# Decoder layer on one core: the row maximum moves into the scores' own contraction, the gate into four column tiles, and TensorE's order becomes a cycle

## What is computed

```python
q = hidden_states @ Wq.T + bq          # k, v alike
scores = einsum('bhqd,bhkd->bhqk', q, k) * SCALE
attn = softmax(where(mask, scores, -inf), axis=-1)
return einsum('bhqk,bhkd->bhqd', attn, v) @ Wo.T + bo
```

```python
gp = softmax(xf @ gate_w.T, axis=-1)           # 8 experts
ew, _ = top_k(gp, 2)
ew = ew / (sum(ew) + 1e-09)
ef = silu(xf @ up_w.T) @ down_w.T              # 1024 wide
out = ef * sum(ew)
```

## Time and profile before

| what | value |
|---|---|
| median of 3 runs | 3605.91 us |
| lowest, highest | 3600.19, 3607.89 us |
| span of the profiled execution | 3601.5 us |
| PE busy | 3488.3 us, 97% of the span |
| DVE, POOL, ACT busy | 77%, 70%, 48% |
| share of PE in the chain that ended last | 93% |

### The profile page before, as it was taken

One profiled execution on the slowest core, in us unless ns is written; L12 is line 12 of the kernel. 1 busy time (PEld: TensorE's weight loads), 2 busy tenths in 40 slices (PEclk: granted clock), 3 DMA queues, 4 the chain that ended last, 5 costly groups with the idle time before them and its releaser, 6 DMA issues.

```text
span 3601.5 us, 97036 instructions
## 1 busy us (share of the span) xinstructions
PE 3488.3 (97%) x38789; PEld 2853.8 (79%) x38789; DVE 2764.0 (77%) x6256; ACT 1715.7 (48%) x4049; POOL 2507.6 (70%) x3159
## 2 busy tenths in 40 slices
PE   6699999999999999999999999999999999999998
PEld 5578888888888888888888888888888888888876
DVE  5677787787787787787787877877877877877863
ACT  2345545545545445445545545445445455455443
POOL 5767777777777677677677777777677677677742
PEclk8899999999999999999999999999999999999999
DMA  5111111111121121121121121111111111111100
GB/s 177 48 50 59 61 67 53 66 69 48 67 72 45 67 74 45 67 74 45 67 74 45 67 73 46 67 67 53 67 63 57 67 60 60 67 57 62 67 8 10
DMA packets 87098, 221.54 MB, mean 62 GB/s; under 512 B 8262, under 2 KB 53634, under 8 KB 70274
## 3 DMA queue, kind: packets, MB, share of 16 engines
q1 hardware_dynamic: 86658, 215.34, 16.9%
HBM read 164.92 MB, written 50.39 MB: 60 GB/s over the span
## 4 chain that ended last, share of the span: by engine, by line
PE 93%; DVE 4%; ACT 2%; issue 1%; POOL 0%; DMA 0%; SPq 0%; DVEq 0%; ACTq 0%
PE ps L869 13%; PE ps L860 13%; PE ps L722 11%; PE ps L700 10%; PE ps L839 9%; PE ps L756 8%; PE ps L811 8%; PE ps L788 6%; PE ps L728 5%; PE ps L680 3%; PE ps L780 3%; PE ps L849 2%; DVE held L1355 1%; PE ps L750 1%; ACT rest L1002 1%; DVE nmax_pair L1292 1%
## 5 line engine op out<-in xcount | busy, mean ns | idle before, releaser
L1124 POOL TENSOR_TENSOR chunks<-v_windows,xT 128x560 f32<-128x560 f32 (+1 forms) x384 | 870.8, 2284 | 259.0 <-DVE xT L1267 155.0
L1292 DVE TENSOR_REDUCE nmax_pair<-ps 128x4 f32<-128x480 f32 (+2 forms) x1280 | 776.1, 669 | 167.8 <-PE ps L756 167.5
L1119 POOL TENSOR_TENSOR chunks<-rest,k_windows 128x512 f32<-128x512 f32 (+1 forms) x384 | 552.9, 1455 | 436.8 <-DVE xT L1246 232.6
L969 ACT ACTIVATE prob<-ps 128x256 f32<-128x256 f32 (+2 forms) x1536 | 670.0, 548 | 331.9 <-PE ps L788 331.9
L860 PE MATMUL ps<-xT,w_up 128*128 128x256 f32 x2048 | 483.7, 384 | 0.0
L869 PE MATMUL ps<-w_down,held 128*128 128x256 f32 x2048 | 458.9, 382 | 1.8 <-DVE held L1355 1.6
L869 PEld LDWEIGHTS ps<-w_down,held 128*128 128x128 f32 x2048 | 383.9, 190 | 72.2 <-issue 20.4
L860 PEld LDWEIGHTS ps<-xT,w_up 128*128 128x128 f32 x2048 | 375.7, 191 | 44.7 <-issue 0.9
L1246 DVE TENSOR_REDUCE xT<-chunks 128x32 f32<-128x512 f32 (+1 forms) x384 | 294.0, 766 | 128.0 <-POOL chunks L1119 128.0
L927 ACT COPY xT<-ps 128x512 f32<-128x512 f32 x256 | 149.8, 585 | 489.3 <-PE ps L680 489.2
L1136 POOL TENSOR_SCALAR_AFFINE_SELECT prob<-prob 128x512 f32<-128x512 f32 x512 | 319.5, 655 | 75.7 <-ACT prob L969 75.7
(11 more groups left out here) (146 smaller groups left out, 6086.6 us busy)
## 6 DMA issues: line engine op xcount, KB each, us to landing
k_windows<-passed_on SPq DMA_DIRECT2D x64, 1024.0 KB, 4.6
v_windows<-passed_on SPq DMA_DIRECT2D x64, 1024.0 KB, 5.1
x<-in_x SPq DMA_DIRECT2D x64, 256.0 KB, 2.9
passed_on<-rest SPq DMA_DIRECT2D x64, 256.0 KB, 2.0
passed_on<-held SPq DMA_DIRECT2D x64, 256.0 KB, 2.0
out<-x SPq DMA_DIRECT2D x64, 256.0 KB, 2.1
y<-in_ctx SPq DMA_DIRECT2D x64, 120.0 KB, 2.8
w_up<-in_up SPq DMA_DIRECT2D x1, 1024.0 KB, 8.8
```

Source lines behind the costliest of these rows:

```text
L969: last = nc.scalar.activation(prob_pair(seq, L, m)[0:keys, :, r, col:col + qs], of_pair, ACT.Exp, scale=SCALE)
L1119: last = nc.gpsimd.tensor_tensor(chunk_of(c).rearrange("p (j d) -> p j d", d=D), q_row, window("k", (b + first) * D, (D, n), (1, D)), ALU. ...
L1124: last = nc.gpsimd.tensor_tensor(chunk_of(c).rearrange("p (h i j) -> p h i j", i=HD, j=WINDOW), window("v", b * D + first * HD, (HD, n), ( ...
L1292: nc.vector.tensor_reduce(nmax[s][:, tb, heads], src, AX_X, ALU.max, negate=True).then_inc(emptied[b], 1)
```

## The change

Per sequence:

- `kT` becomes two tiles for each attention, one per e: rows of the other head are scaled to zero by `half`, and one of these empty rows is set to 1 by a bias (`one_row`, or `bias_k[e]`). ACT writes k twice: 2 instructions instead of 1 for the causal k, 4 instead of 2 for the cross k.
- The matmuls with `pick` are gone, and with them `round_max`, its bf16 tiles and the constant. `shift` now transposes the fp32 maxima (128x16 in, 16x128 out), DVE copies 16 rows of 256.
- A new SP step `place` copies these rows by two DMAs (8 rows of 1 KB each) into the empty row of each quarter of `qT[e]`. `scores` waits for both. So the negated maximum enters as the 17th row of the fp32 contraction; the matmuls k by q stay as many and as large as they were.
- `gate` has the weights as its stationary operand, 32 columns in each of four column tiles, and streams 64 tokens through each: 8 matmuls for 4. DVE turns the result with a transpose instead of a copy.
- `Plan` orders PE's steps by `POSITION`, a number for each step within a cycle plus the number of the sequence; PE takes the next step of that line and no other, except at the ends (`FILLING`, `LOOKS`). The other engines' steps are due by the PE steps that follow them, shifted by `SHIFTED`. The two first score units of a layer may not be taken between those of another.

```diff
-DELAY = {("gate", None, "PE"): 55, ("project", 2, "PE"): 2975, ("project_out", 1, "PE"): -85,
...
+POSITION = {("turn", (0,)): -0.0773, ("turn_ctx", ()): -0.0394, ("project_rows", ("k",)): -0.0389, ("project_rows",
...
+            a = through("shift", (layer,), 0.2, "DVE", 0.4, last)
+            shifted = part("place", (layer,), "SP", 2 * DMA_ISSUE, [a], lag=2.0)
...
-            ready[parts[i].engine].append((SENIORITY * n - left[i] + delay[i], n, i))
...
+        line = sorted((n + due[i], n, i) for n, i in todo if parts[i].engine == "PE")
...
+                    elif name == "place":
+                        L, = args
+
+                        wait_taken(sp, "shift", seq, L)
+                        for e in range(2):
+                            to = qT[s][e][16 * (1 - e):P:32]
+                            sp.dma_start(to, nmaxT[s][8 * e:8 * e + 8, :]).then_inc(placed[s], 16)
...
-                        to = ps[:, b, :].bitcast(BF16)
                         for tb in range(2):
-                            last = nc.tensor.transpose(to[:, tb * P:(tb + 1) * P], nmax_parts[s][:, tb, :],
-                                                       ident_b[:])
+                            last = nc.tensor.transpose(ps[0:H, b, tb * P:(tb + 1) * P], nmax[s][:, tb, :], ident[:])
...
-                        wait_taken(pe, "shift", seq, L)
+                        pe.wait_ge(placed[s], reached["placed", "place", seq, (L,)])
...
-                                nc.tensor.matmul(ps[0:keys, to[r], n * qs:(n + 1) * qs], pick[rows, g, 0:keys],
-                                                 nmaxT[s][rows, q0:q0 + qs], start=(n == 0), stop=False,
-                                                 tile_position=(32 * r, 0), skip_group_check=True)
...
-                                                        kT[s][rows, m, key0:key0 + keys],
-                                                        qT[s][e][rows, m, q0:q0 + qs], start=False, stop=True,
+                                                        kT[L][s][e][rows, m, key0:key0 + keys],
+                                                        qT[s][e][rows, m, q0:q0 + qs], start=(n == 0), stop=True,
...
-                        for tb in range(2):
-                            for k in range(2):
-                                last = nc.tensor.matmul(ps[:, b, tb * E:(tb + 1) * E],
-                                                        xT[s][:, k, tb * P:(tb + 1) * P], w_gate[:, k, :],
-                                                        start=(k == 0), stop=(k == 1))
+                        for k in range(2):
+                            for j in range(4):
+                                tokens = xT[s][:, k, :].rearrange("p (b j i) -> p j b i", b=2, i=SLOT)[:, j]
+                                last = nc.tensor.matmul(ps[SLOT * j:SLOT * (j + 1), b, 0:2 * SLOT], w_gate[:, k, :],
+                                                        tokens, start=(k == 0), stop=(k == 1),
+                                                        tile_position=(0, SLOT * j), skip_group_check=True)
...
-                            last = nc.scalar.copy(kT[s], ps[:, b, :].rearrange("p (m t) -> p m t", m=2))
+                            for e in range(2):
+                                last = nc.scalar.activation(kT[L][s][e], ps[:, b, :].rearrange("p (m t) -> p m t", m=2),
+                                                            ACT.Identity, bias=one_row[:, e:e + 1],
+                                                            scale=half[:, e:e + 1])
```

More of the change, by code:

```diff
@@ L72 @@
 PLACES = {"lane": LANES, "prob": PROBS, "k_window": 1, "v_window": 1, "chunks": 1}
[L74 to L88 removed]
+DIVIDED = {"max": "rows", "scores": "rows", "values": "columns", "gate": "columns"}
@@ L112, in setup_parts @@
     part("derive", ("tables",), "DVE", 1.4, [tables], (), banks)
[L113 to L114 removed]
+    part("derive", ("half",), "DVE", 0.9, [])
+    part("derive", ("bias",), "DVE", 4.6, [loads[3], ("derive", ("half",), "DVE")])
     part("derive", ("scale",), "DVE", 4.3, [loads[3], loads[4]])
@@ L249 @@
            ("scores", "POOL"): {"masked": 1},
-           ("round_max", "DVE"): {"nmax_ready": 1},
+           ("place", "SP"): {"placed": 32},
            ("normalise", "DVE"): {"attended": 1},
@@ L258 @@
 BY_WEIGHT = ("sent", "fetched")
-BY_LAYER = ("moments", "norm", "turn", "project", "max", "round_max", "shift", "scores",
+BY_LAYER = ("moments", "norm", "turn", "project", "max", "shift", "place", "scores",
             "values", "normalise", "project_out")
@@ L510, in decoder @@
         loaded = [sem(f"loaded{n}") for n in range(len(LOADS))]
-        derived = {what: sem(f"derived_{what}") for what in ("pick", "bias", "scale", "cross", "causal")}
+        derived = {what: sem(f"derived_{what}") for what in ("half", "bias", "scale", "cross", "causal")}
         filled = [sem(f"filled{b}") for b in range(BANKS)]
```

241 lines of the change are left out of this document (129 added, 112 removed).

## The result

| what | before | after |
|---|---|---|
| median, lowest, highest (us) | 3606.9, 3600.19, 3611.71 | 3525.09, 3522.85, 3526.76 |
| span of the profiled execution | 3601.5 | 3523.7 |
| first `down` starts at | 218.7 | 217.7 |
| 59 cycles | 3207.9 | 3124.3 |
| from the 60th `down` to the end | 174.9 | 181.7 |

The changed kernel takes 0.977 of the time (95% interval 0.976 to 0.979): 82 us less. Faster was forecast, but with 3456 us, and a range that ended at 3500. The result lies 25 us outside it. About 55% of the forecast gain came. (The spans of the two profiled executions differ by 78: 1.0 ahead of the first `down`, 83.6 in the cycles, 6.8 lost behind them.)

A forecast was written before the change was run, and what follows sets the result against it. PE was taken as the bound, plus fill and drain. Terms summed to 2.4 us a cycle (52.0), 141.6 over 59 cycles; with drain 8 and fill 1, 150 less: span 3451.5, median 3456 us, range 3428 to 3500.

The forecast's parts named there:

- The gate: Gate step in column tiles: 0.35 us in place of 0.91, a gain of 0.55 a cycle (0 to 0.7).
- The borders and their count: Each group of divided steps costs 0.3 us beside its work; 6 groups for 7, gain 0.2 to 0.3.
- The placed row: First unit of a layer waits for DVE's copy and two DMAs: 2.4 us for the DMAs, 1.4 margin, so no cost.
- Matmuls with pick ... I take 1.2: In five score units: the removed bf16 matmuls save 1.2 us a cycle, bounds 0.6 and 1.3.
- 0.25 for what the bf16 to fp32 change cost: Inside score units and behind `shift`: the change of type no longer costs, a further gain of 0.25 us a cycle.
- The rival "cover": Bf16 matmuls hid the first fp32 weight loads, so `pick` brings 0.6, type changes nothing: 3511 us, chance 0.1.
- So 0.05 us is left there: Bank wait behind `project_out` and a unit in the new order: 0.92 us needed, 0.87 filled, 0.05 waited.
- some 0.15 until PE sees it: Bank wait: time from DVE's emptying of the bank until PE goes on, put at 0.15 us.
- three such places: Whole-array step, unit, four-bank `max`: there and behind `project_rows` k and q, new waits 3 x 0.05 us a cycle.
- The old wait of 0.5: At the last score units before: 0.5 us of waiting goes; net 0.35 a cycle after the new waits.
- The prediction's sign for this: If the cycle is longer, PE's list of waits names the rival; no waits at all means cover.
- the drain "about 8" less: Behind the steady cycles: the rest of four sequences runs at PE's pace, saving about 8 us.

The follow-up runs named there:

- e2_cover: Changed kernel with bf16 matmuls on zeros put back ahead of each score unit's fp32 matmuls, which overwrite their result: 3551.9 us, ratio 0.985.
- e11_before_no_pick: Kernel before, in its own order, with the matmuls with `pick` left out and nothing in their place: 3585.39 us, ratio 0.994.
- e1_late_last: Changed kernel with PE's waits for four banks sorted so the bank filled last is waited for last: 3504.81 us, ratio 0.972.
- e3_gate_whole: Changed kernel with the gate as before, four whole-array matmuls copied by DVE, order unchanged: 3568.42 us, ratio 0.989.
- The experiments on filling: Changed kernel with sorted bank waits and `FILLING` 3 or 9 in place of 6: 3517.98 us and 3515.35 us.
- e4_max_first: Changed kernel with two positions changed, so each cross score unit stands behind the four-bank `max`, not ahead: 3560.87 us, ratio 0.987.

## Why the prediction was wrong, step by step

The span was forecast at 3451.5 and is 3523.7, a miss of 72 us: some 51 in all cycles (0.87 x 59), 7 more in the first two, 15 at the ends.

*The bound, the sign, the lesser terms: right.* PE stayed the bound, at 99.8% of the steady stretch. The gate came at 0.34 for 0.35. Its neighbour row (columns set the price) was the right end to lean on; the rule of the Trainium skill, TensorEngine Tiling (Array Packing), "Instruction Overhead", left the gain standing for 64 columns, and the trace agrees. `shift` cost 0.22 as forecast. The borders and their count hold too: a whole-array step costs 1.73 between its like and 1.82 or 1.83 beside a divided one, as before, and `values (1)`, with no whole-array step behind it, fell by 0.12. The change from the gate's column tiles to the row tiles of `(2, 1)` costs no more than a unit's first half costs behind a whole-array step (0.54 and 0.53). So "Key Properties" of the same page (a change of mode drains TensorE) agrees with the price of borders; a drain of 0.3 inside a group is not there. The placed row was never waited for in the steady part, once for 2.9 us in the fill: forecast to land 2.4 us after the first issue, it took 2.2, with 1.9 us of margin for 1.4.

*The first step that failed: "Matmuls with pick ... I take 1.2", and with it the "0.25 for what the bf16 to fp32 change cost".* Together they put 1.4 us on the five units; by the parts of a unit, e2_cover and e11_before_no_pick measure 0.8. The bf16 matmuls did cover something. The first eight fp32 records of a unit behind a whole-array or column-tiled step cost 0.53 without them and 0.43 with them. The text had this as a possibility and set two things against it: that steps that begin with fp32 after bf16 gain nothing visible, and that the fp32 part costs 0.86 "whatever stands ahead". In both rows that it names bf16 matmuls stand ahead, so neither says what happens without them. `max (1, 1)` of the kernel before, at 1645.49, would have: it begins with fp32 behind a whole-array step and pays 0.10. The prediction did not look there, and 1.2 lay near its upper bound of 1.3. The second term was wrong in its sign for the units: with bf16 ahead, fp32 began cheaper, not dearer. (Behind `shift` it was right: that `up` fell from 1.78 to 1.73.) Four first halves at 0.10 and 0.02 in `(2, 2)` make 0.4 us, the change of type that never was 0.2. The rival "cover" was right in kind, and its 3511 us are the nearest of the priced cases to 3525; its 0.6 for all five lies between the 0.8 of the parts and the 0.4 by which a cycle moved.

*The second: "So 0.05 us is left there", "some 0.15 until PE sees it", and three such places.* From the emptying of the bank to PE it takes 0.36 us at the step that waits, not 0.15, where the last filled bank stands first among four waits. The forecast 0.15 a cycle became 0.46, at four steps (`scores (1, 0)` 0.24, `(1, 1)` 0.06, `max (1, 0)` 0.07 and `(1, 1)` 0.09, by what each lost in e1_late_last). The old wait of 0.5 at `scores (2, 0)` did go, as forecast; 0.06 are left there. e1_late_last shows it: the same work and the same waits in another order are 0.3 us a cycle shorter. The prediction's sign for this failed too: PE's list of waits names none in the steady part, which was to mean cover alone, and a third of the miss was waits all the same.

*Together* that is 0.6 and 0.3, against a miss of 0.92 in units and `max` steps. Of the 1.53 us that a cycle did gain, the gate is 0.73 (e3_gate_whole) and `pick` 0.4 (e2_cover); the other 0.4 is left for the new order, which no run measures alone. Two small sums of the prediction are off and change nothing: 0.1 + 0.69 + 0.15 is 0.94 and not 0.92, and 0.06 for each of five units and a `shift` is 0.36, where 0.25 was taken.

*The third: the drain "about 8" less.* It grew by 6.8 us, with PE busy 3 us longer and granted a lower mean clock (0.94 for 0.98). Also the first two cycles took 56.67 and 55.63 us. The forecast gave the rest of four sequences PE's pace and did not look at how the new order uses the engines there. The later half of this stretch, and a part of it, with the columns of the earlier trace rows:

```profile
3430.00:3523.70 93.70, 74.22 (x634) 57.67 (x632) 30.37 (x71) 29.61 (x80) 21.39 (x46) 0.90 0.03 10
3491.30:3504.90 13.60, 8.24 (x22) 5.90 (x21) 2.38 (x6) 2.09 (x4) 2.54 (x5) 0.50 0.00 0
```

PE is busy 79% of it, at a clock of 0.90, and 19.5 of the stretch's 25 us of idle PE stand here. Of the 6.8 us, 2.9 are PE's busy time and 3.9 its idle time. The second row is a stretch at the lower level, 1.2 GHz: PE had idled 2.45 us just ahead of it and idled 4.59 inside it, and two of the last sequence's `up` steps, which take 3.55 us in the steady cycles, took 6.5 across it. These 3 us match the busy time that was added. Why PE waits there longer than the old order did (none of its waits in this stretch is over 2 us) stays open. The experiments on filling moved the loss of the first cycles and did not take it away, so its cause stays open too.

What the 0.10 of a first group is made of was not tested apart, but the traces bear on it. In a `max` of the causal layer the mask's bf16 matmuls (0.12 us) stand ahead, already in row tiles, and the first eight fp32 records still take 0.51 us where the next take 0.43 in e4_max_first, where no border follows. So the change to row tiles is not all of it; a cover too short for the load of the fp32 weights would look like this. No run changed the size or type of the weights alone, so that is argued and not shown.

*The range.* It was built from single terms at their better or worse bound, and did not take both of these at once. Cover alone, at 3511, lay outside it, with a chance of 0.1.

## What to carry to other kernels

What a step costs is read from rows in which it stands behind the same kind of neighbour, and a fp32 part that follows bf16 matmuls is no price for one that doesn't. Cheap work in front of such a part may be cover that gives back a share of what it costs (0.10 of 0.26 us here). Where an instruction of PE waits for several semaphores, let the one that comes last be waited for last: this took a few lines here and gave 20 us; in the order of before it gave nothing. An order with fixed positions must be weighed together with its ends: here the first cycles and the drain took back 13 of the 90 us that the cycle gained.

## What the runs showed of the chip

- PE's sequencer works off waits that don't fit on an instruction as instructions of their own (51 ns long, some 0.1 us apart) ahead of the next weight load. Satisfied waits that stand behind the one that comes last cost 0.06 to 0.24 us a step here; ahead of it, nothing that shows. The list of PE's waits shows none of it: it stands as idle PEld ended by "issue".
- The first eight fp32 records (256 columns each) of a row-tiled step behind a whole-array or column-tiled one cost 0.53 us; the following eight 0.43. With eight bf16 records (0.26 us) ahead, or behind another row-tiled fp32 step, the first eight cost 0.43 too (once 0.48).
- A fp32 transpose of 128 x 16 costs 0.11 us; 16 records of 64 columns in column tiles cost 0.34 us together.
- A DMA of 8 or 2 KB from SBUF to SBUF costs SP 0.55 or 0.60 us to issue, and the last one's data were there for PE 1.06 us after its issue. By the Trainium skill, DMA: Bandwidth & Descriptors, "Anatomy of one DMA", about 2.0 us are fixed; that section is on DMAs that GpSimd issues, and these are SP's. The 2.0 us row that the prediction set beside it holds the transfer of 256 KB as well, so it does not show the fixed part. Here one took 1.6 us from the start of its own issue (0.55 + 1.06), and the two 2.2 from the start of the first.
